# A two-layer graph kernel: another order of its first and last stage, and a fifth source block of each row split by VectorE

## What is computed

```python
node = h @ W1                                   # 128 -> K = 16
hw = einsum('nc,kcf->nkf', h, W2)
x0 = einsum('nk,nkf->nf', node, hw)
x1 = layernorm(x + relu(adj @ x0 + node @ b))
msg = x1 @ W + B
weights = where(adj < 1, exp(-(1/adj - 1)**2 / 0.5), 0)
out = layernorm(x1 + weights @ msg)
```

## Time and profile before

| | |
|---|---|
| median of 3 runs | 622.33 us |
| the profiled execution | 621.25 us, of which 619.5 us are the span from first to last instruction |
| busy share of the span | PE 92%, DVE 83%, ACT 81%, POOL 14% |
| first stage, to the last x0 | 0 to about 122 us |
| row 0, and row 1 until the column tiles run | 122 to 203 us |
| rows with both kinds of tile | 203 to 534 us |
| closing, column tiles and output | 534 to 619.5 us |

### The profile page before, as it was taken

One profiled execution on the slowest core, in us unless ns is written; L12 is line 12 of the kernel. 1 busy time (PEld: TensorE's weight loads), 2 busy tenths in 40 slices (PEclk: granted clock), 3 DMA queues, 4 the chain that ended last, 5 costly groups with the idle time before them and its releaser, 6 DMA issues.

```text
span 619.5 us, 5187 instructions
## 1 busy us (share of the span) xinstructions
PE 570.8 (92%) x1746; PEld 324.7 (52%) x1746; DVE 514.4 (83%) x561; ACT 503.4 (81%) x529; POOL 86.4 (14%) x72
## 2 busy tenths in 40 slices
PE   6999899788789999999999999999999999967994
PEld 5777677454455555555555555555555555532441
DVE  5999999699789888989988898898889888667621
ACT  3677667468867997999799799979997997999833
POOL 2778787700000000000000000000000000000000
PEclk9999999989899999999999999999999999988997
DMA  5592100098469788888878888788888775451011
GB/s 158 227 423 81 34 2 0 5 369 322 153 239 335 276 320 305 307 295 306 313 290 330 316 293 315 291 314 311 294 303 336 293 284 175 165 203 68 17 53 68
DMA packets 24523, 142.26 MB, mean 230 GB/s; under 512 B 2704, under 2 KB 4912, under 8 KB 8112
## 3 DMA queue, kind: packets, MB, share of 16 engines
q1 hardware_dynamic: 23824, 141.65, 61.6%
q10 hardware_dynamic: 672, 0.27, 0.2%
HBM read 139.81 MB, written 2.10 MB: 229 GB/s over the span
## 4 chain that ended last, share of the span: by engine, by line
PE 64%; ACT 15%; DVE 13%; issue 6%; DMA 1%; POOL 1%; POOLq 0%; ACTq 0%; DVEq 0%
PE l_ps L371 29%; PE acc_ps L336 13%; DVE part_acc L553 6%; ACT wt L447 4%; ACT wt L452 4%; PE acc_ps L329 4%; PE acc_ps L327 4%; PE acc_ps L328 4%; DVE x_hi L532 2%; PE hw_ps L307 2%; ACT wt L457 2%; ACT wt L464 2%; PE hw_ps L308 2%; PE hw_ps L309 2%; ACT wt L467 2%
## 5 line engine op out<-in xcount | busy, mean ns | idle before, releaser
L371 PE MATMUL l_ps<-wt,msg 128*128 128x512 f32 x512 | 232.4, 598 | 4.6 <-DVE msg L617 4.6
L371 PEld LDWEIGHTS l_ps<-wt,msg 128*128 128x128 f32 x512 | 97.5, 192 | 120.8 <-issue 113.2
L447 ACT ACTIVATE wt<-wt 128x2048 f32<-128x2048 f32 x64 | 121.5, 1898 | 39.6 <-DVE wt L585 39.6
L585 DVE SCALAR_TENSOR_TENSOR wt<-wt 128x2048 f32<-128x2048 f32 x64 | 146.1, 2283 | 0.0
L591 DVE SCALAR_TENSOR_TENSOR wt<-wt 128x2048 f32<-128x2048 f32 x40 | 91.6, 2289 | 42.1 <-ACT wt L452 42.1
L452 ACT ACTIVATE wt<-wt 128x2048 f32<-128x2048 f32 x64 | 122.5, 1915 | 2.0
L336 PE MATMUL acc_ps<-row_in,x 128*128 128x512 f32 x256 | 115.2, 592 | 0.0
L438 ACT ACTIVATE prods<-hw_ps,node 128x128 f32<-128x128 f32 x256 | 73.2, 369 | 36.9 <-PE hw_ps L309 22.1
L464 ACT ACTIVATE wt<-wt 128x2048 f32<-128x2048 f32 x40 | 75.8, 1896 | 8.1 <-DVE wt L591 8.1
L694 POOL TENSOR_TENSOR prods<-prods 128x1024 f32<-128x1024 f32 (+2 forms) x48 | 74.8, 1558 | 34.2 <-ACT prods L438 31.7
L336 PEld LDWEIGHTS acc_ps<-row_in,x 128*128 128x128 f32 x256 | 48.5, 190 | 59.2 <-issue 58.8
(11 more groups left out here) (57 smaller groups left out, 404.9 us busy)
## 6 DMA issues: line engine op xcount, KB each, us to landing
row_in<-adjT_dram SPq DMA_DIRECT2D x64, 1024.0 KB, 6.8
wt<-adjT_dram SPq DMA_DIRECT2D x64, 1024.0 KB, 4.8
x_in<-xT_dram SPq DMA_DIRECT2D x8, 256.0 KB, 3.8
x_row<-xT_dram SPq DMA_DIRECT2D x8, 256.0 KB, 5.8
outT_dram<-sumT SPq DMA_DIRECT2D x8, 256.0 KB, 2.0
W_in<-W_dram SPq DMA_DIRECT2D x3, 256.0 KB, 5.4
W_in<-W_dram ACTq DMA_DIRECT2D x1, 256.0 KB, 5.1
B_sb<-B_dram SPq DMA_DIRECT2D x1, 256.0 KB, 4.9
```

Source lines behind the costliest of these rows:

```text
L371: mm = pe.matmul(l1_ps[:, t % L1_BANKS, :], msg[:, c % 2, k, :], wt[t % WT_RING][:, k, :], start=(k == 0), stop=(k == CH - 1))
L447: act.activation(w[:, :, :], w[:, :, :], ACT.Ln, bias=TINY).then_inc(ln_made, 1)
L585: dve.scalar_tensor_tensor(out=w, in0=w, scalar=1.0, in1=w, op0=ALU.is_lt, op1=ALU.mult).then_inc(mask_made, 1)
```

## The change

Both ends are put in another order, and one more source block is split. At the start ACT makes the high part of x, POOL the low part, ACT the high part of x0, and DVE the low part of x0 only in the steps behind; W2 comes in a layout in which each partition reads one run; `sumT` is no longer cleared, its first writers copy. `exp_step` is even from 0 for the first six tiles, which ACT squares itself; the last six tiles stand at steps of their own and are all squared by DVE. A square on DVE now comes one step later (`exps_at.get(i - 1)`). Row 0 splits source blocks 3, 5, 7, every later row 1, 3, 5, 6, 7. At the end the last two output blocks are centred into other banks, and `square2` goes before `inverse_root2`.

```diff
-SPLIT = (1, 3, 5, 7)
+SPLIT = (1, 3, 5, 6, 7)
+SPLIT_FIRST = (3, 5, 7)
+FIRST_EVEN = 6
+LAST_EVEN = 58
+LAST_STEPS = (66, 67, 69, 70, 72, 73)
...
     def exp_step(m):
-        return 2 * m + 1 if m < 6 else m + COL_LAG - 5
+        if m < FIRST_EVEN:
+            return 2 * m
+        return m + COL_LAG - 5 if m < LAST_EVEN else LAST_STEPS[m - LAST_EVEN]
...
     def is_split(i):
-        return i % NB in SPLIT
+        return i % NB in (SPLIT if i >= NB else SPLIT_FIRST)
...
     def on_dve(m):
+        if m < FIRST_EVEN or m >= LAST_EVEN:
+            return m >= LAST_EVEN
         return m % NB in DVE_SQUARED
...
-                at_least(pe, out_made, j - 1)
-                pe.matmul(acc_ps[:, j % 2, :], centre_w[:, :], block_of(sumT, j), start=True,
+                if j < NB - 2:
+                    at_least(pe, out_made, j - 1)
+                pe.matmul(yc2_ps[j], centre_w[:, :], block_of(sumT, j), start=True,
                           stop=True).then_inc(yc2_made, 1)
...
+            def round_x(g):
+                s = g % 2
+                act.wait_ge(x_in_sem[s], 16 * (g // 2 + 1))
+                for half in range(2):
+                    at_least(act, hw_made[half], (g - 1) * GROUPS)
+                act.activation(x_hi[:, s, :], x_in[:, s, :], ACT.Copy).then_inc(x_hi_made, 1)
...
+                    if n == 0 and g + 1 < NB:
+                        round_x(g + 1)
                     if n == GROUPS - 3 and g + 1 < NB:
                         copy_node(g + 1)
+                    if n == GROUPS - 2 and g - 1 in SPLIT:
+                        round_x0(g - 1)
...
-                    if q == 1 and g + 1 < NB:
-                        round_x(g + 1)
...
-            dve.wait_ge(fold_step, NB * FOLDS)
-            for i in range(SPLIT_LEAD):
-                if is_split(i):
-                    split_row_tile(i)
-            if NB - 1 in SPLIT:
-                split_x0(NB - 1)
+            mask(0)
...
                 if i + SPLIT_LEAD < TILES and is_split(i + SPLIT_LEAD):
+
+                    while remainders and remainders[0] <= (i + SPLIT_LEAD if i + SPLIT_LEAD < NB else NB):
+                        remainder_of_x0(remainders.pop(0))
                     split_row_tile(i + SPLIT_LEAD)
...
-                for t in exps_at.get(i, []):
+                for t in exps_at.get(i - 1, []):
                     if on_dve(t):
                         take_square(t)
...
+            def remainder_of_x(g):
+                s = g % 2
+                pool.wait_ge(x_hi_made, g + 1)
+                pool.tensor_tensor(x_lo[:, s, :], x_in[:, s, :], x_hi[:, s, :], ALU.subtract).then_inc(x_lo_made, 1)
...
             for g in range(NB):
+                if g + 1 < NB:
+                    remainder_of_x(g + 1)
                 fold(g)
```

More of the change, by code:

```diff
@@ L124, in gnn_kernel @@
         with ExitStack() as first:
-            node = sb("node", [P, 2, CH, K], F32, first)
+            W2_in = sb("W2_in", [P, K, P], F32, first)
+            W2_hi = sb("W2_hi", [P, K, P], F32R, first)
+            W2_lo = sb("W2_lo", [P, K, P], F32R, first)
             x_in = sb("x_in", [P, 2, BW], F32, first)
@@ L128, in gnn_kernel @@
             x_lo = sb("x_lo", [P, 2, BW], F32R, first)
+            prods = sb("prods", [P, HALF, K, P], F32, first)
+            node = sb("node", [P, 2, CH, K], F32, first)
             part_acc = sb("part_acc", [P, HALF, P], F32, first)
-            W2_in = sb("W2_in", [P, K, P], F32, first)
-            W2_hi = sb("W2_hi", [P, K, P], F32R, first)
-            W2_lo = sb("W2_lo", [P, K, P], F32R, first)
-            prods = sb("prods", [P, HALF, K, P], F32, first)
-        wt += [sb(f"wt_{s}", [P, CH, BW]) for s in range(WT_RING - LATE_SLOTS, WT_RING)]
         if SPLIT:
@@ L138, in gnn_kernel @@
             adj_lo = [sb(f"adj_lo_{s}", [P, CH, BW], F32R) for s in range(2)]
+        wt += [sb(f"wt_{s}", [P, CH, BW]) for s in range(WT_RING - LATE_SLOTS, WT_RING)]
         y = sb("y", [P, BW])
@@ L154, in gnn_kernel @@
         msg_ps = var_ps.rearrange("p (c f) -> p c f", f=P)
+        yc2_ps = [acc_ps[:, j % 2, :] if j < NB - 2 else l1_ps[:, j % 2, :] for j in range(NB)]
         var2_ps = [yc_ps, var_ps]
@@ L223, in load_row_tile @@
                 if before >= 0 and is_split(before):
-                    sp.wait_ge(adj_lo_made, splits_before(before) + 1)
+                    sp.wait_ge(adj_lo_made, split_tiles.index(before) + 1)
                 elif before >= 0:
@@ L483, in square2 @@
                 at_least(act, var2_made, j - 1)
-                act.activation(sq[:, j % 2, :], acc_ps[:, j % 2, :], ACT.Square).then_inc(sq2_made, 1)
+                act.activation(sq[:, j % 2, :], yc2_ps[j], ACT.Square).then_inc(sq2_made, 1)
             def inverse_root2(j):
@@ L509, in _ @@
                     take_inverse(t)
+                if i == 0 and NB - 1 in SPLIT:
+                    round_x0(NB - 1)
                 for t in left:
@@ L608, in add_row, with last_part @@
                 if r == 0:
-                    dve.wait_ge(sum_cleared, 1)
-                at_least(dve, sum_added, (r - 1) * NB + r + 1 if r + (r - 1) * NB <= NB * r - 3 else (r - 2) * NB + r + 1)
+                    dve.tensor_copy(block_of(sumT, r), x1T[:, :]).then_inc(x1_added, 1)
+                    return
+                dve.wait_ge(sum_added, last_part(r) + 1)
                 dve.tensor_tensor(block_of(sumT, r), block_of(sumT, r), x1T[:, :], ALU.add).then_inc(x1_added, 1)
+            def last_part(r):
+                return max(t for t in range(r, TILES, NB) if t + COL_LAG + 1 <= NB * (r + 1) + 2)
             def copy_messages(r):
@@ L621, in add_part @@
                 dve.wait_ge(col_tile_done, t + 1)
+                if t == j and j > 0:
+                    dve.tensor_copy(block_of(sumT, j), l1_ps[:, t % L1_BANKS, :]).then_inc(sum_added, 1)
+                    return
                 at_least(dve, sum_added, t - NB + 1)
@@ L637, in finish @@
                 dve.wait_ge(rstd2_made, j + 1)
-                dve.tensor_tensor(block_of(sumT, j), acc_ps[:, j % 2, :], rstd[:, j % 2, :],
+                dve.tensor_tensor(block_of(sumT, j), yc2_ps[j], rstd[:, j % 2, :],
                                   ALU.mult).then_inc(out_made, 1)
-            round_x(0)
-            for q in range(QUARTERS):
+            split_W2(0)
+            first_remainder_of_x()
+            for q in range(1, QUARTERS):
                 split_W2(q)
```

66 lines of the change are left out of this document (27 added, 39 removed).

## The result

The changed kernel takes 633.17 us (median of 4 runs, 633.04 to 634.68), the kernel before 621.66 beside it (4 runs, 620.83 to 623.09): a ratio of 1.0188, with an interval of 1.0162 to 1.0215. It is slower by 1.6 to 2.2%, where the forecast said a little faster, and 2.2 us outside its range. The profiled execution has a span of 631.5 us against 619.5.

What follows compares the result with a forecast made beforehand. PE was taken to bound the steady rows before the change, a DVE-ACT-PE ring after it. Span 619.5 - 10.5 (ramp) + 20.5 (rows) - 12.2 (closing) = 617.3, with 1.75 outside it 619.0 us; range 610 to 631.

Steps and rivals of the forecast that it cites:

- the first case: Whole kernel: the ring closes as worked out and PE's clock holds, 619.0 us, own range 613 to 625; chance 0.52.
- the ring: Steady rows: DVE, ACT and PE wait in a circle that closes once per row, 59.2 us against PE's 55.06.
- the last fold: Seam after the first stage: POOL ends it at about 110.6 us, so SP's loads go out 12.1 us earlier.
- rival 2: Steady rows: PE's clock falls to half at the new waits, 628 to 638 us; chance 0.17.
- the sign that I had named for this rival: Steady rows: residuals over 60.5 us apart, with PE's clock below 1.00, would show the clock falling.
- First stage, -13: First stage: blocks take 11.9 us instead of 13.56, so it ends at 103.2 instead of 116.2.
- Ramp to row 1, -10.5: Start to the residual of row 1: at about 192.3 us instead of 202.76.
- Rival 3: Steady rows: they follow PE at 55.06 us each, 594 us in all; chance 0.08.
- Neither edit alone reaches PE's time by much: Steady rows: late square alone gives 55.7 us; only together do both edits add 3.5 us to each row.
- Closing, -12.2: From the residual of row 7 to the end: 73.3 us instead of 85.5, trusted within 4 us.
- last row: Row before the residual of row 7: its last steps split nothing, so 59.2 - 3.47 = 55.7 us.

Runs made afterwards that it cites:

- dummy: Changed kernel plus two unused PE matmuls per row from the second, ahead of its wait for the residual; 626.73 us.
- mix58seam: Changed kernel with four splits, late square only for column tiles 58 to 63, and DVE waiting for POOL's last fold before its first mask; 597.72 us.
- late5b4: Changed kernel, late squares throughout, with the fifth split of block 4 instead of block 6; 618.2 us.
- late4: Changed kernel with the fifth split taken back (blocks 1, 3, 5, 7), late squares kept; 615.44 us.
- early5: Changed kernel with DVE's squares back in their own step, one earlier, all five splits kept; 625.24 us.

## Why the prediction was wrong

The step that failed is the clock: the first case has "the clock holds", with PE waiting some 2.5 us in the ring once per row. PE waited 2.2 us, its clock fell after five of six such waits, and that is some 8 of the 14.2 us. The second is the price of the last fold, about 3.

- **The clock, rival 2 with 0.17, decided.** I let it begin "from a wait between these two on", 2.59 that held and 3.61 that fell. It fell after 2.2 us, in five of six cases, and rows over 60.5 us with a clock below 1.00, the sign that I had named for this rival, are three of the five between rows 1 and 6. `dummy` prices it: four rows are 1.7 us shorter there and the closing 1.4, 8.2 us; the medians, 633.17 less 626.73, plus the 1.6 that its matmuls cost in row 1, give 8.0. Without it the time would have been some 625, inside the range, but still 0.5% over the kernel before: the other 6 us are more than the 2.2 by which the forecast lay under it, so the sign was lost without the clock too. (The first stage's waits of 1.47 us, which the forecast sets against this rival, are seven, not eight.)
- **First stage, -13: right.** The last hidden product ends at 102.8 us (103.2 forecast, 116.2 before).
- **Ramp to row 1, -10.5: mis-sized, it is -6.5.** What failed is "POOL ends its last fold at about 110.6": I let DVE and POOL work side by side at the price that each has alone. The fold ended at 113.1 and the loads followed at 113.21. The delay goes through the ramp as forecast: row tile 5 is there at 127.76 (124.5 forecast), ACT has done tiles 2, 3 and 4 at 156.6 (153.2), and the residual of row 1 is 3.9 us late. That taking DVE away brings the loads forward is shown in `mix58seam`; in the changed kernel itself it was not tried. The two lines of the changed kernel's DVE and ACT timelines:

```profile
127.76 1.23 DVE L586 CAST adj_hi<-row_in 128x2048 fp32r<-128x2048 f32 x1 [9.67 <-DMA row_in<-adjT_dram]
```

```profile
154.66 1.91 ACT L484 ACTIVATE wt<-wt 128x2048 f32<-128x2048 f32 x1
```

- **The ring, 59.2: right.** The rows with full clock are 59.35 long, the wait for the root is 4.07 (some 4 forecast), those of PE 2.2 and 1.6 (2.5 and 1.8). Rival 3, rows at PE's pace, is out, and with it what the rule that stood beside the forecast would give here (the Trainium skill, Perfetto Trace Analysis, section Identifying the Most-Contended Engine): the fifth split took work from the engine with the highest occupancy, and no row became shorter by it; they became 0 (`late5b4` against `late4`) to 1.8 us longer. For TensorE that section wants its headroom judged by other measures than busy time; I did not look at those.
- **"Neither edit alone reaches PE's time by much": wrong.** Late square alone 57.55 (55.7 forecast), fifth split alone 57.32 (53.0 by the same sum, 49.5 + 3.47). I had followed one ring and subtracted from it. Behind it stood a second through the messages and, in the early order, a third over masks and inverses. It did not touch the forecast's number, since with both edits the first ring is the longest, but it is why I expected too little of `late4` and `early5`.
- **Closing, -12.2: nearly right as a size (-9.9, of which the clock took 1.4), wrong in its reason.** The forecast followed the queues of the changed kernel, the late squares among them, but names only the new order as what gives; that alone gives nothing, the late square alone 1.7 us, and only both 10 to 12.
- **The sum.** Of the 14.2 us, some 8 are the clock's and about 3 the contended fold's; the rest is spread over ramp, ring, last row and closing, under 1 us each. Gains of the ends and loss of the rows were each 20 us: a small result of large terms, whose sign an error of 2 us in one of them can turn.

## What to carry to other kernels

Read a stage that three engines share as a set of rings, not one: before an instruction is moved, list every way from an engine's wait back to the same instruction a round later, and take the longest for each version, also for each edit alone. The same edit can be right in one stage and wrong in another; split it by stage before judging it (with the new closing the late square costs 1.8 us a row here and gives 11 to 14 us at the end; only at the end, with four splits and the fold waited for, it is part of 597.7 us where the kernel before takes 622.2). A new wait of TensorE inside a ring is to be priced with its clock, even if an equal one elsewhere in the trace was free; here two matmuls into a bank that is overwritten anyway gave 6.4 us back. And a difference at one point of one profile is to be held against kernels that are alike up to that point, before it is called an effect.
